# Deformable convolution kernel: mask multiplied into the row hats, two images per y tile, sums copied out by ScalarE, x rows six units ahead

## What is computed

```python
om = conv3x3(gn(x), w_om) + b_om            # 108 rows: 36 dy, 36 dx, 36 masks (4 groups x 9 taps)
py = row - 1 + ki + dy                      # per group, tap and position
px = col - 1 + kj + dx
v = bilinear(gn(x), py, px) * sigmoid(mask) # four neighbours, weights (1-wy)(1-wx), ...
out = x + relu(einsum("ogck,bgckhw->bohw", w_dcn, v))
```

## Time and profile before

| what | value |
|---|---|
| three executions | 206.64, 208.68, 205.33 us |
| the profiled execution's own time | 204.33 us |
| its span | 202.2 us |
| TensorE busy | 160.4 us (79%) |
| VectorE busy | 142.8 us (71%) |
| ScalarE busy | 95.7 us (47%) |
| GpSimd busy | 85.8 us (42%) |
| DMA queue of SyncE | 26.87 MB, 49.5% of 16 engines |
| mean granted TensorE clock | 0.97 |

### The profile page before, as it was taken

One profiled execution on the slowest core, in us unless ns is written; L12 is line 12 of the kernel. 1 busy time (PEld: TensorE's weight loads), 2 busy tenths in 40 slices (PEclk: granted clock), 3 DMA queues, 4 the chain that ended last, 5 costly groups with the idle time before them and its releaser, 6 DMA issues.

```text
span 202.2 us, 3958 instructions
## 1 busy us (share of the span) xinstructions
PE 160.4 (79%) x1546; PEld 102.8 (51%) x1546; DVE 142.8 (71%) x243; ACT 95.7 (47%) x149; POOL 85.8 (42%) x108
## 2 busy tenths in 40 slices
PE   0598869979899199299996953999797887969980
PEld 0235436443375034056685742646665676747770
DVE  3899889965693559444996864643999596986930
ACT  1165096100009694249675277447918493973000
POOL 8609963694200066022916324520843528444000
PEclk9999999999999969859999999999999999999998
DMA  5700000000503949992859999449539679470001
GB/s 170 277 18 2 3 0 0 3 0 0 104 3 73 289 131 254 242 279 74 222 167 237 270 238 257 108 126 250 169 89 251 191 206 275 140 218 3 18 0 23
DMA packets 12963, 27.19 MB, mean 134 GB/s; under 512 B 2238, under 2 KB 5386, under 8 KB 12938
## 3 DMA queue, kind: packets, MB, share of 16 engines
q1 hardware_dynamic: 12938, 26.87, 49.5%
HBM read 22.80 MB, written 1.44 MB: 120 GB/s over the span
## 4 chain that ended last, share of the span: by engine, by line
PE 28%; DVE 22%; DMA 19%; ACT 10%; POOL 8%; issue 6%; SPq 4%; DVEq 0%; POOLq 0%
PE ps L1335 10%; DMA hx<-placed_rows 8%; PE ps L1309 6%; PE ps L1272 4%; DMA placed_rows<-x_placed 4%; DVE smp_prod L888 4%; DMA disty<-placed_rows 3%; DVE smp_prod L914 3%; POOL haty L599 3%; DVE smp_prod L1020 3%; DMA kept<-in_cf 3%; PE ps L1204 3%; ACT hx L738 3%; ACT disty L728 2%; PE ps L1378 2%
## 5 line engine op out<-in xcount | busy, mean ns | idle before, releaser
L1020 DVE TENSOR_TENSOR smp_prod<-ps,hx 128x768 f32<-128x768 f32 x72 | 65.6, 949 | 3.5 <-ACT hx L740 1.8
L1335 PE MATMUL ps<-smp_prod,windows_attention 128*64 128x192 f32 (+2 forms) x512 | 53.6, 337 | 2.7 <-DMA windows_attention<-windows_attention 2.3
L1309 PE MATMUL ps<-haty,by_rows 128*64 128x256 f16 x432 | 37.5, 280 | 16.1 <-POOL haty L599 10.2
L592 POOL TENSOR_SCALAR disty<-disty 64x512 f32<-64x512 f32 (+1 forms) x23 | 13.3, 577 | 74.4 <-ACT haty L731 73.5
L1335 PEld LDWEIGHTS ps<-smp_prod,windows_attention 128*64 128x64 f32 x512 | 36.8, 137 | 9.4 <-DMA windows_attention<-windows_attention 2.6
L1309 PEld LDWEIGHTS ps<-haty,by_rows 128*64 128x64 f16 x432 | 23.9, 111 | 29.3 <-DVE smp_prod L1020 15.8
L738 ACT ACTIVATE hx<-hx,offset 128x768 f32<-128x768 f32 x24 | 22.3, 930 | 29.4 <-DMA hx<-placed_rows 29.3
L1032 DVE TENSOR_TENSOR vals_attw<-ps,windows_attention 128x384 f32<-128x384 f32 x24 | 13.3, 555 | 21.0 <-PE ps L1335 21.0
L1272 PE MATMUL ps<-conv_staged 128*112 128x512 f32 (+1 forms) x60 | 25.7, 561 | 0.1
L599 POOL TENSOR_TENSOR haty<-disty,haty 64x512 f16<-64x512 f32 (+1 forms) x23 | 24.9, 1083 | 1.9
L740 ACT ACTIVATE hx<-hx 128x768 f32<-128x768 f32 x24 | 20.3, 844 | 0.8
(11 more groups left out here) (133 smaller groups left out, 193.4 us busy)
## 6 DMA issues: line engine op xcount, KB each, us to landing
hx<-placed_rows SPq DMA_DIRECT2D x24, 384.0 KB, 5.4
disty<-placed_rows SPq DMA_DIRECT2D x7, 640.0 KB, 5.5
windows_attention<-placed_rows SPq DMA_DIRECT2D x16, 192.0 KB, 3.2
windows_attention<-placed_rows SPq DMA_DIRECT2D x16, 160.0 KB, 3.4
windows_attention<-windows_attention SPq DMA_DIRECT2D x8, 256.0 KB, 6.8
placed_rows<-x_placed SPq DMA_DIRECT2D x3, 224.0 KB, 3.8
x_placed<-in_x SPq DMA_DIRECT2D x2, 256.0 KB, 3.0
x2seq<-x_placed SPq DMA_DIRECT2D x4, 128.0 KB, 2.5
```

What stands on the lines that cost most here:

```text
L592: nc.gpsimd.tensor_scalar(d, d, 1.0, 0.0, ALU.min, ALU.max).then_inc(s_uy, 1)
L1020: nc.vector.tensor_tensor(pairs, rows, cols.unsqueeze(1).to_broadcast([P, QUARTERS, HW]), ALU.mult).then_inc(s_mult, 1)
L1309: ins = nc.tensor.matmul(ps[h * C:(h + 1) * C, at:at + HW], by_matrix(a, QUARTERS - 1 - k)[:, h * C:(h + 1) * C], haty[i % 2][:, p * HW:(p ...
L1335: return nc.tensor.matmul(dst[:, at:at + strips * 3 * SP].rearrange("p (s k n) -> p s k n", k=3, n=SP), rows, sampled(i, ki, m, first, str ...
```

## The change

- The convolution's result rows are now 36 x rows, 40 y rows and 40 mask rows in the y rows' layout (116 rows). All are written to `placed_rows` together, for every piece; `write_mask` and `masks` go.
- Y rows and masks are loaded over 64 partitions an image. `JOBS` groups the images (0), (1), (2,3), (4,5), (6,7): an even image lies in partitions 0-63, an odd one in 64-127 of the same tile, so that one ScalarE operation works for two images. Masks go to a tile `masky` of the same layout, which has one buffer.
- GpSimd multiplies the hat (now fp32 in place) by the mask for a job (`masked_y`), then copies it to fp16 and subtracts, for each image (`low_y`: two operations instead of three).
- `values` becomes a plain copy, and moves from VectorE to ScalarE, at steps 8, 1 and 4 behind the other work of the step.
- `hx` has six slots. The x rows of the first three units are issued before the first odd pairs, those of units 3 to 5 behind them; the very first 256 columns are loaded from ScalarE's queue, and have hats of their own (`first_hat_x`).
- In the start ScalarE takes tanh straight from PSUM ahead of the raw offsets (`mask_rows`, `raw_offsets`), VectorE normalises two of four images of `tall` before the first placement, and the placement of piece 2 and the convolution of piece 3 move one or two steps back.

```diff
-HX = 4
+HX = 6
+JOBS = [(0,), (1,), (2, 3), (4, 5), (6, 7)]
+YBUF, YFREE, MFREE = [0, 0, 1, 0, 1], [-6, -6, 0, 6, 12], [0, 0, 6, 9, 12]
-PLACE_AT, AMAX_AT = {(0, 1): 2, (1, 0): 3, (4, 0): 4}, {(0, 2): 2, (1, 1): 3, (4, 1): 4}
+PLACE_AT, AMAX_AT = {(0, 3): 2, (1, 0): 3, (4, 0): 4}, {(0, 4): 2, (1, 1): 3, (4, 1): 4}
-SEL_Y = {2: 0, 6: 1, 8: 2}
+SEL_Y = {2: 0, 5: 1, 8: 2}
...
+            def expand_y(n, it):
+                reach(sp, s_loy, YFREE[n], it)
+                for i in JOBS[n]:
+                    y_rows(i, ND, disty, YBUF[n] * YI, 0, YI, s_yrows[n])
+            def expand_masks(n, it):
+                reach(sp, s_masked, MFREE[n], it)
+                for i in JOBS[n]:
+                    y_rows(i, SHIFTED, masky, 0, 0, YI, s_mrows[n])
+            def y_rows(i, first, t, at, lo, hi, signal):
+                sp.dma_start(t[lanes(i), at + lo:at + hi],
+                             rows_of(i, first + lo // HW, [[0, WROWS], [YI, 2 * DG], [1, hi - lo]])).then_inc(signal, 16)
...
             write(0)
             sp.wait_ge(s_wrote[0], 16)
-            expand_y(0, 0, HW, s_yfirst, 0)
-            expand_x(0, 0)
-            expand_y(0, HW, YI, s_yrows[0], 0)
+            y_rows(0, ND, disty, 0, 0, HW, s_yfirst)
+            y_rows(0, SHIFTED, masky, 0, 0, HW, s_mfirst)
+            y_rows(0, ND, disty, 0, HW, YI, s_yrows[0])
+            x_rows(sp, 0, HW, UW, s_xrows[0])
+            y_rows(0, SHIFTED, masky, 0, HW, YI, s_mrows[0])
+            write(1)
             expand_x(1, 0)
-            write(1)
+            sp.wait_ge(s_wrote[1], 16)
+            expand_y(1, 0)
+            expand_masks(1, 0)
             expand_x(2, 0)
-            for p in range(DIRECT):
-                write_mask(p)
...
             odd_pairs(0)
-            for i in range(B):
+            for u in range(UNIT, HX):
+                expand_x(u, 0)
+            for i in range(B - 2):
...
+            def masked_y(n, e, it):
+                reach(pool, s_haty, 3 * n + e + 1, it)
+                reach(pool, s_mrows[n], 16 * len(JOBS[n]), it)
...
+                nc.gpsimd.tensor_tensor(y, y, m, ALU.mult).then_inc(s_masked, 1)
             def low_y(i, e, it):
...
+                reach(pool, s_by, STEPS * (i - 1), it)
+                reach(pool, s_masked, 3 * n + e + 1, it)
...
+                nc.gpsimd.tensor_copy(hats[high], y).then_inc(s_high, 1)
+                nc.gpsimd.tensor_tensor(hats[low_], y, hats[high], ALU.subtract).then_inc(s_loy, 1)
...
+            def values(i, part, it):
+                reach(act, s_chunk, CHUNK * i + part + 1, it)
...
+                nc.scalar.copy(vals[:, part * w:(part + 1) * w], bank(6 if part == 1 else 7)[:, 0:w]).then_inc(s_vals, 1)
...  # ScalarE, in sampling
-                    if m in SEL_Y and i + 1 < B:
-                        distance_y(i + 1, SEL_Y[m], it)
+                    if m in SEL_Y and i + 1 < B and JOBS[JOB[i + 1]][0] == i + 1:
+                        distance_y(JOB[i + 1], SEL_Y[m], it)
...
                     if (i, m) == (LAST_CONV, 4) and isinstance(it, int):
-                        offsets(4)
+                        raw_offsets(4)
+                        mask_rows(4)
+                    if m == 8:
+                        values(i, 0, it)
+                    if m == 1 and i:
+                        values(i - 1, 1, it)
+                    if m == 4 and i:
+                        values(i - 1, 2, it)
...  # VectorE, in sampling
-                    if m == 8:
-                        values(i, 0, it)
-                    if m == 1 and i:
-                        values(i - 1, 1, it)
-                    if m == 4 and i:
-                        values(i - 1, 2, it)
```

More of the change, by code:

```diff
@@ L264, in by_image, with cols_of, x_rows, lanes @@
             return t.rearrange("r (i n) -> r i n", n=HW)
[L266 to L278, removed]
+        def cols_of(u, lo=0, hi=UW):
+            return hx[:, u % HX * UW + lo:u % HX * UW + hi]
+        def x_rows(queue, u, lo, hi, signal):
+            i, k = divmod(u, UNIT)
+            queue.dma_start(cols_of(u, lo, hi), rows_of(i, UNIT * k + lo // HW, [[0, 2 * W], [TAPS * HW, DG], [1, hi - lo]])
+                            ).then_inc(signal, 16)
+        def lanes(i):
+            return slice(0, C) if i % 2 == 0 else slice(C, P)
+        def of_job(n):
+            return slice(0, P) if len(JOBS[n]) == 2 else lanes(JOBS[n][0])
+        def y_slice(n, e):
+            return disty[:, YBUF[n] * YI + YP[e] * HW:][:, 0:YW[e]]
         s_x = [sem("s_x0"), sem("s_x1")]
@@ L381, in _ @@
             at, width = kept.shape[1] - 5 - 1, cf.shape[1]
[L382 to L386, removed]
+            constant(bom[0:ND, :], cf[2 * ND, at:at + 1], [[width, ND], [1, 1]])
+            for n in range(2):
+                for a in range(2):
+                    to = ND + (2 * n + a) * DG * PAIRS
+                    constant(bom[to:to + DG * PAIRS, :], cf[(1 - n) * ND + a, at:at + 1],
+                             [[TAPS * width, DG], [2 * width, PAIRS], [1, 1]])
             sp.wait_ge(s_x2, 2)
@@ L491, in _ @@
                     send(i - 1)
+                expand_x(HX + UNIT * i + 2, 0)
+                if i == 0:
+                    expand_masks(2, 0)
+            for i in range(B - 2, B):
+                sp.wait_ge(s_y, i)
+                send(i - 1)
             sp.wait_ge(s_y, B)
@@ L961, in _, with normalise_tall @@
             dve.wait_ge(s_zero, 7)
-            for j in range(J):
+            def normalise_tall(j):
                 normalise(tall[:, :].rearrange("p (j r c) -> p j r c", j=J, r=TROWS)[
@@ L1010, in multiply @@
                 reach(dve, s_by, t + 1, it)
-                reach(dve, s_hatx, t // UNIT + 1, it)
+                if t == 0 and isinstance(it, int):
+                    dve.wait_ge(s_hatfirst, 1)
+                else:
+                    reach(dve, s_hatx, t // UNIT + 1, it)
                 if m >= 3:
```

318 lines of the change are left out of this document (155 added, 163 removed).

## The result

The changed kernel takes 216.91 us, the median of four runs (213.75 to 221.01). The kernel before, run beside it, takes 205.99 us (205.03 to 208.68). The ratio is 1.046, with a 95% interval of 1.035 to 1.058. The forecast was 193.6 us, 188 to 201, with 0.06 for slower: wrong in sign.

What follows compares the result with a forecast made beforehand. From 103 us, DMA and TensorE were nearly balanced, with TensorE kept waiting mostly by late x rows. Waits 13.8 + image 0 2.5 - image 3 1.8 - kept back 1.5 = 13.0 us off 206.64: 193.6 us, range 188 to 201.

Steps and rivals of the forecast that it cites:

- Transfers: Loads per image: 1,792 KB instead of 2,496, 7.1 us at 253 GB/s, under TensorE's 10.4; half-width loads taken at 239 GB/s.
- x rows: From 103 us, six slots and a shorter queue remove ScalarE's 25.7 us wait and TensorE's 9.9 us behind GpSimd.
- Rival (4): ScalarE: x rows still late, sums' copies behind them, `final` inherits the wait, +11.6 less 2.5; 215.7 us, chance 0.06.
- The text's last sentence: ScalarE: prediction fails if it, now serving both sides, waits for products and makes hats too late; no size given.
- Rival (1): Y and mask loads: half-width at 0.6 of the rate, +3.0 us in the first two images; 196.6 us, chance 0.12.
- GpSimd: Low parts: about 7 us an image before and after, priced at nothing; TensorE's wait for it under 2 us.
- rival (2): GpSimd stays behind: waits return at images 2, 4 and 6, each 0.6 us longer; 199.9 us, chance 0.11.
- Sums to ScalarE: Copies leave VectorE, TensorE regains 1.6 us; ScalarE 8.6 of 10.4 us an image, priced at nothing except +1.8 in image 3.
- Image 0: First image, up to its end: window copies come earlier, 2.5 us gained, between 0 and 5; finished near 102.5.
- rival (3): Image 0: TensorE idles in short pieces, clock 0.50 over 20 us loses 8 us, gain absent; 204.1 us, chance 0.11.
- The sum: Whole kernel: 13.8 + 2.5 - 1.8 - 1.5 = 13.0 us saved, giving 193.6 us from the median of 206.64.

Runs made afterwards that it cites:

- e2: Kernel before, each y load over 128 partitions cut into two over 64 with outermost length 8, same bytes; 219.18 us, ratio 1.068.
- e5: Changed kernel, y rows and masks in own DRAM tensors, one 128-partition load of length 16 per image pair, writes of 40, 40, 36 rows; 196.08 us, ratio 0.950.
- e1: Changed kernel, each write of 116 placed rows cut into transfers of 112 and 4 rows; 211.56 us, ratio 1.033 to the kernel before.
- e4: Changed kernel with two mask buffers, masks issued right behind the same job's y rows; 213.53 us, ratio 1.040 to the kernel before.
- e6: e5 with two mask buffers and masks issued right behind the y rows; 193.67 us, ratio 0.942 to the kernel before.
- e3: Kernel before, each x load over 128 partitions cut into two over 64 with outermost length 16, same bytes; 207.12 us, ratio 1.004.
- e9: e5 with the changes of e6 and e8, and image 3's values copy ahead of piece 4's offsets and masks; 186.68 us, ratio 0.907.
- e7: e5 with the sums' copies moved back to VectorE as plain copies; 197.08 us, ratio 0.961 to the kernel before.
- e8: e5 with SyncE's first loads reordered: unit 2's x rows before image 1's write wait, units 3 to 5 before odd pairs; 192.16 us, ratio 0.937.

## Why the prediction was wrong, step by step

**Transfers: the step that failed.** It counted bytes and took one rate for all of them, 239 GB/s for the half-width form, read from the stretch 73.9 to 78 us. That row shows loads over 64 partitions with an outermost length of 16. The new ones have 8, and none of the rows read shows such a load. A load of 8 runs on 8 of the 16 engines (e2 and the count of packets). The shape of the source pattern stood in the diff, and only the number of partitions was read from it. With theory A as an estimate: of an image's 1,792 KB, engines 0 to 7 carry half of the x rows (576 KB) and all of the y rows and masks (640 KB), 1,216 KB. At half of 253 GB/s that is 9.6 us, where the forecast had 7.1 and the kernel before 9.9: by this estimate the smaller transfer saved next to nothing. What was measured is masks landing 13.3 to 14.9 us after issue, TensorE waiting 10.9 us behind them where under 2 were forecast, and 20.8 us (19.8) given back by e5 with the same bytes.

**Writes.** The step had no term for them. 112 rows (76 and 36 for the first two pieces) became 116; cut into 112 and 4 they were cheaper by 5.3 us (2.7), a size within the noise (e1).

**The single mask buffer** was not priced either. Before, masks were used last, in the sums' copies, from two buffers. Now they are used first, ahead of the hats, from one. The prediction let y jobs begin "three in a row, 3.1 us against 2.5, begun earlier", and didn't ask when the masks of that job could be issued. It is worth 1 to 3 us (e4, e6), never clear of noise, small beside the rate but in the same place.

**x rows** went as forecast: the wait from 103 us is gone, though a landing took 8.5 us, not 5.4. Six slots cover it. Rival (4), which had the right sign and nearly the right number (215.7), named x rows and ScalarE; neither was late. But its way of passing a delay on is there, with y rows in the place of x rows: 4.56 us of waiting on ScalarE became 4.21 ahead of `final`, once. The text's last sentence had said so of ScalarE; the price that was put on it was nothing, because every load was held to be in time.

**Rival (1)** was nearest in its cause: half-width loads slower than taken. It had the cause as the width (refuted by e3) and the rate as 0.6, and still gave 196.6. Applied to 640 KB alone it was too mild because loads on eight engines also hold up half of each x load behind them (8.6 us to land in e2).

**GpSimd**, rival (2), is what the profile after seems to say: TensorE waits for it at every pair. But GpSimd was idle in front, waiting for masks. With them in time, TensorE's wait is 2.1 us (e5) and 1.2 us (e9): the forecast's "under 2" for the work itself. The mask product took 1.275 us for 128x512, taken as 1.21.

**Sums to ScalarE**: the copy of 384 took 0.477 us, taken as 0.5. Priced at nothing for each image, and e7 against e5 shows 1.0 us (2.2), no difference that can be told. Of TensorE's 7.8 us ahead of `final`, 4.2 are behind the late y rows, 1.4 are in image 1, and 2.2 are in image 3, where 1.8 on top of 0.3 were forecast (e5 has the same 2.2).

**Image 0**: forecast 2.5 us sooner, measured 7 later. The step placed units 3 to 5 behind the odd pairs and took unit 2 as there. It goes out behind the wait for piece 1's write, and both were late here. The writes cost image 0 some 3.4 us (112.01 in after, 108.57 in e1) and the order some 5.5 (109.57 in e5, 104.08 in e8), each from one profile; TensorE's clock (0.63 from 75 to 90 us, 0.81 before) follows from the gaps, rival (3) in part.

**The sum.** From the changed kernel to the forecast: 20.8 us for form and writes (e5) and 2.4 for the buffer (e6) lead to e6's 193.67 us, where 193.6 was forecast. That is partly luck: image 0 is 6.5 us later than forecast in e6, and TensorE's periods (10.05) are shorter than the 10.4 taken.

**Left open:** which eight and which four engines they were; whether the place in DRAM has a part in e5; how much of image 0's 7 us is the clock; the size of what the writes and the mask buffer cost.

## What to carry to other kernels

Before costing a transfer, write down the outermost length of both its sides, and take a rate only from a row with the same one: 8 in place of 16 turned a saving of 28% of the bytes into a loss, and partitions alone said nothing. When a load moves from late use to early use, price the moment at which its buffer comes free, not only its length. And when an engine waits for another that is itself idle, follow the chain one step more before calling that engine the bound.

## What the runs showed of the hardware

The outermost length of a load decided its rate more than its partitions: y loads in two of length 8 cost the kernel before 6.8% (e2), x loads in two of length 16 cost 0.4%, within its interval of none (e3). The counts of packets and of semaphore steps give the reason: 16 for a transfer of length 16, 32 or 112, 8 for one of 8, 4 for one of 116 or 76. Five writes of 116 rows in place of 112 and 4 cost 5.3 us by the medians and 2.7 by the ratios, within the intervals. The packets themselves took little longer: the profile gives those of the main queue 49.5% of a span of 202.2 us for 26.87 MB before, and 38.7% of 215.2 for 21.00 MB after, 3.7 and 4.0 us of all 16 engines for a MB. While y rows or masks moved alone, the DMA share was 0.47 and 0.48: half of the engines had nothing to do. A share near 1 is no proof of the contrary, as 0.92 at 188 GB/s shows. And transfers of this form are seen in the views by what is missing: they print no landing. (e1's writes of 112 rows print none either, because they share a semaphore with those of 4.)
